# Outputs on four column tiles, values copied over the head's partitions by DMA

## The reference

```python
def step(state, inp):
    r_t, d_t, k_t, v_t, a_t, b_t = inp
    sa = jnp.einsum('bhij,bhj->bhi', state, a_t)
    state = state * d_t[:, :, None, :] + sa[..., None] * b_t[:, :, None, :] + v_t[..., None] * k_t[:, :, None, :]
    return (state, jnp.einsum('bhij,bhj->bhi', state, r_t))
```

## Time and profile before

| | |
|---|---|
| median of 3 runs | 1345.38 us (1345.16 to 1351.12) |
| profiled execution, span | 1345.0 us |
| instructions | 18208 |
| PE, PEld busy | 1145.7 us (85%), 648.0 us (48%) |
| DVE busy | 978.8 us (73%) |
| ACT busy | 708.3 us (53%) |
| POOL busy | 615.8 us (46%) |
| DMA | 12 GB/s over the span |
| mean granted TensorE clock | 0.962 |
| first `s_a` (L884), last `state` | 67.22 us, 1251.8 us |
| a chunk in the loop, from its first `s_a` to the next chunk's | 76.8 to 78.3 us |

### The profile page before, as it was taken

One profiled execution on the slowest core, in us unless ns is written; L12 is line 12 of the kernel. 1 busy time (PEld: TensorE's weight loads), 2 busy tenths in 40 slices (PEclk: granted clock), 3 DMA queues, 4 the chain that ended last, 5 costly groups with the idle time before them and its releaser, 6 DMA issues.

```text
span 1345.0 us, 18208 instructions
## 1 busy us (share of the span) xinstructions
PE 1145.7 (85%) x4848; PEld 648.0 (48%) x4848; DVE 978.8 (73%) x2366; ACT 708.3 (53%) x1087; POOL 615.8 (46%) x869
## 2 busy tenths in 40 slices
PE   3576778999898989989799979999898998989896
PEld 1244545555545545555455545455454555555432
DVE  2477888879696968879497877969587887958311
ACT  1544446466564636466464545656355655634454
POOL 0145555555455545555355544545455554545100
PEclk9888879999999989999899999999899999989998
DMA  2000000000000000000000000000000000000000
GB/s 112 0 9 17 1 16 1 4 14 8 16 1 25 1 25 0 8 16 8 16 0 24 0 24 0 8 16 0 24 0 24 0 16 0 17 1 17 0 9 16
DMA packets 7442, 16.61 MB, mean 12 GB/s; under 512 B 956, under 2 KB 956, under 8 KB 7240
## 3 DMA queue, kind: packets, MB, share of 16 engines
q1 hardware_dynamic: 7368, 15.84, 3.4%
HBM read 11.65 MB, written 4.19 MB: 12 GB/s over the span
## 4 chain that ended last, share of the span: by engine, by line
PE 40%; DVE 36%; issue 18%; ACT 4%; DMA 1%; DVEq 1%; SPq 0%; POOL 0%; ACTq 0%; POOLq 0%
DVE state L898 7%; DVE upd L894 6%; PE sa_ps L360 6%; PE o_ps L353 5%; PE fin_a L541 5%; PE pre_a L311 3%; PE pre_b L311 3%; DVE s_a L884 3%; PE fin_b L541 3%; PE vb_ps L311 3%; PE mid_ps L311 3%; PE mid_ps L495 2%; DVE kv L872 2%; DVE y L1046 2%; PE fin_a L311 1%
## 5 line engine op out<-in xcount | busy, mean ns | idle before, releaser
L1094 POOL TENSOR_TENSOR plus_kv<-state,kv 128x128 f32<-128x128 f32 x512 | 285.4, 557 | 578.5 <-DVE state L898 542.2
L360 PEld LDWEIGHTS sa_ps<-s_a,con 128*128 128x128 f32 x1024 | 174.6, 196 | 387.6 <-DVE s_a L884 332.8
L360 PE MATMUL sa_ps<-s_a,con 128*128 128x128 f32 x1024 | 233.0, 311 | 122.1 <-DVE s_a L884 114.9
L894 DVE TENSOR_TENSOR upd<-sa_ps,b_t 128x128 f32<-128x128 f32 x512 | 144.8, 283 | 179.9 <-PE sa_ps L360 179.2
L1087 POOL TENSOR_TENSOR s_r<-state,r_t 128x256 f32<-128x256 f32 x256 | 218.6, 854 | 1.0 <-DVE state L898 1.0
L898 DVE TENSOR_TENSOR state<-upd,plus_kv 128x128 f32<-128x128 f32 x512 | 153.7, 300 | 17.6
L884 DVE TENSOR_TENSOR s_a<-state,a_t 128x128 f32<-128x128 f32 x512 | 149.3, 292 | 17.7
L353 PE MATMUL o_ps<-s_r,con 128*128 128x128 f32 x1024 | 142.4, 285 | 1.5 <-POOL s_r L1087 1.5
L541 PE MATMUL fin_b<-h_e,mat 128*128 128x512 f32 x256 | 129.6, 604 | 7.6 <-ACT pick L776 6.8
L353 PEld LDWEIGHTS o_ps<-s_r,con 128*128 128x128 f32 x1024 | 131.7, 201 | 1.7 <-POOL s_r L1087 1.7
L541 PE MATMUL fin_a<-h_e,mat 128*128 128x512 f32 x256 | 122.1, 593 | 0.0
(11 more groups left out here) (185 smaller groups left out, 2021.0 us busy)
## 6 DMA issues: line engine op xcount, KB each, us to landing
x_in<-xT SPq DMA_DIRECT2D x16, 256.0 KB, 2.7
x_res<-xT SPq DMA_DIRECT2D x16, 256.0 KB, 2.8
outT<-res SPq DMA_DIRECT2D x16, 256.0 KB, 2.0
mat<-mats SPq DMA_DIRECT2D x1, 2306.0 KB
con<-consts SPq DMA_DIRECT2D x1, 840.0 KB, 4.3
hid<-b SPq DMA_DIRECT2D x3, 8.0 KB
vec<-vecs SPq DMA_DIRECT2D x1, 11.5 KB, 4.5
```

The costliest lines, as they stand in the source:

```text
L360: mm(sa_ps[:, 0:STATE], k("sum8"), s_a[:], start=True, stop=True).then_inc(s["sa"], 1)
L894: tt(ib(upd[:]), ib(sa_ps[:, 0:STATE]), over_i(b_t[c.slot][:, t * B:(t + 1) * B]), ALU.mult).then_inc(s["upd"], 1)
L1094: tt(plus_kv[:, (t % 2) * STATE:(t % 2 + 1) * STATE], st(t), kv[:, at:at + STATE], ALU.add).then_inc(s["plus_kv"], 1)
```

## The change

The partitions of everything behind the scan are ordered by value, then head (i times 16 plus h), by permuting columns and rows of the weights on the host, and the head's mean is taken off in the weights of a second form of v and no longer in `gather`.

- Outputs: `gather` becomes 32 columns wide; the matmuls of the values 2p and 2p+1 write the 32 partitions of column tile p of `o_ps`, the even value with `start`, the odd one with `stop`. All eight matmuls are in step 3 of the next quarter.
- Values: `pre` makes a centered v with channels on the partitions by one 512-column matmul (`val_scan`, made in the fill), and ACT copies it to `val_c`. SP issues, for each quarter, eight SBUF-to-SBUF DMAs, one for each value i: 16 partitions of `val_c` read eight times each, written to 128 partitions of `val_rep`, 64 KB. DVE's `kv` reads `val_rep` in SBUF. ACT's `replicate`, PE's `spread` and the waits of `vb_free` are gone. v for the bonus is made by a second 512-column matmul.

```diff
+for _name, _w in [("center", C), ("mean", C), ("mean8", C), ("center8", C), ("sum8", C), ("sum8v", C), ("ident", C),
+                  ("gather", N * 32), ("rank", 4 * E)]:
...
+        val_rep = [sb(f"val_rep{n}", N * QCOLS) for n in range(2)]
+        val_scan = sb("val_scan", C)
+        val_c = sb("val_c", COLS)
...
 # SP
+            def replicate(c, q):
+                slot, turn = q % 2, q // 2
+                free = c.count(2 * (q - 2) + 2, 2 * QUARTERS)
+                if not isinstance(free, int) or free > 0:
+                    sp.wait_ge(s["kv"], settled(sp, free))
+                if q == 0:
+                    sp.wait_ge(s["val_c"], settled(sp, c.count()))
+                for i in range(N):
+                    heads = val_c[i * H:(i + 1) * H, q * QCOLS:(q + 1) * QCOLS].unsqueeze(1).broadcast_to([H, N, QCOLS])
+                    sp.dma_start(val_rep[slot][:, i * QCOLS:(i + 1) * QCOLS], heads).then_inc(s[f"val_rep{slot}"], 16)
+
+            def pre(c):
+                yield 17
+                replicate(c, 0)
+                yield 18
+                replicate(c, 1)
+
+            def scan(c):
+                yield 1
+                replicate(c, 2)
+                yield 8
+                replicate(c, 3)
...
-            pipeline(nc.sync, fill, [(2, norm), (-1, mid), (-3, last_norm)], None, finish)
+            pipeline(nc.sync, fill, [(2, norm), (1, pre), (0, scan), (-1, mid), (-3, last_norm)], None, finish)
...
 # PE, fill
+                nc.tensor.transpose(fin_b[:, 0:C], w("W_v"), k("ident")).then_inc(s["wv_turned"], 1)
+                pe.wait_ge(s["wv_sb"], 1)
+                mm(fin_b[:, C:2 * C], val_scan[:], k("center8"), start=True, stop=True,
+                   skip_group_check=True).then_inc(s["wv_c"], 1)
+                pe.wait_ge(s["wv_sb"], 2)
...
 # PE, outputs
-                for n in range(N // 2):
-                    i = half * N // 2 + n
-                    last = mm(o_ps[:, q * QCOLS:(q + 1) * QCOLS], k("gather", i), part[:, i],
-                              start=(i == 0), stop=(i == N - 1), skip_group_check=True)
-                if half:
-                    last.then_inc(s["o"], 1)
+                for odd in range(2):
+                    for pair in range(N // 2):
+                        i = 2 * pair + odd
+                        last = mm(o_ps[32 * pair:32 * pair + 32, q * QCOLS:(q + 1) * QCOLS], k("gather", i, 32),
+                                  part[:, i], start=(odd == 0), stop=(odd == 1), skip_group_check=True)
+                last.then_inc(s["o"], 1)
...
 # PE, scan step
-                if at in (1, 2) and nxt[0].has():
...
-                    spread(*nxt, at - 1)
-                if at in (3, 4) and done[0].has():
-                    outputs(*done, at - 3)
+                if at == 3 and done[0].has():
+                    outputs(*done)
...
 # PE, pre
-                for n in range(QUARTERS):
-                    last = mm(pre_a[:, n * C:(n + 1) * C], mix["v"][:, n * QCOLS:(n + 1) * QCOLS], w("W_v"),
-                              start=(n == 0), stop=True, skip_group_check=True)
-                last.then_inc(s["v"], 1)
+                one(pre_a[:], val_scan[:], mix["v"][:], "v")
...
-                pe.wait_ge(s["val_tm"], c.count())
-                for n in range(QUARTERS):
-                    last = nc.tensor.transpose(pre_a[:, n * QCOLS:(n + 1) * QCOLS],
-                                               val_tm[c.slot][:, n * C:(n + 1) * C], k("ident"))
-                last.then_inc(s["vt"], 1)
+                pe.wait_ge(s["val_c"], c.count())
+                one(pre_a[:], w("W_v"), mix["v"][:], "val_mm")
...
 # ACT
-                if at in (0, 1) and nxt[0].has():
-                    replicate(*nxt, at)
...
-                f(val_tm[c.slot][:], pre_a[:], ACT.Identity).then_inc(s["val_tm"], 1)
+                if c.has(1):
+                    act.wait_ge(s["val_rep0"], (c + -1).count(32 * N, 32 * N))
+                    act.wait_ge(s["val_rep1"], (c + -1).count(32 * N, 32 * N))
+                f(val_c[:], pre_a[:], ACT.Identity).then_inc(s["val_c"], 1)
...
 # DVE, spread_kv
-                dve.wait_ge(s["vb"], c.count(2 * q + half + 1, 2 * QUARTERS))
+                dve.wait_ge(s[f"val_rep{q % 2}"], c.count(16 * N * (q // 2 + 1), 32 * N))
...
+                values = val_rep[q % 2][:, half * N // 2 * QCOLS:(half + 1) * N // 2 * QCOLS]
+                values = values.rearrange("p (i t b) -> p i t b", i=N // 2, t=QUARTER)
...
-                tt(part, vb_ps[:].rearrange("p (i t b) -> p i t b", i=N // 2, t=QUARTER),
+                tt(part, values,
                    keys.unsqueeze(1).broadcast_to([128, N // 2, QUARTER, B]), ALU.mult).then_inc(s["kv"], 1)
```

More of the change, by code:

```diff
@@ L194, in build @@
         res = single("res", COLS)
-        sa_ps, o_ps, vb_ps = bank("sa_ps"), bank("o_ps"), bank("vb_ps")
+        sa_ps, o_ps, var_ps = bank("sa_ps"), bank("o_ps"), bank("var_ps")
         pre_a, pre_b, mid_ps, fin_a, fin_b = (bank(n) for n in ("pre_a", "pre_b", "mid_ps", "fin_a", "fin_b"))
@@ L201, in build @@
         names = """x_in x_res stored consts_in w_in consts_ready
-            wo_turned wo_sb wo_c bo_c c0 sq0 j0 ln0 rs0 xh0 x1 x1_keep c1 sq1 j1 ln1 rs1 xh1 xn carry dx mix_w mix_a mix_k mix_v mix_r mix_g
-            w1 th_w a1 low_a k key v val_tm val_rep vt val r rec g1 th_g w2 th_d a2 th_a dec cum p inv_p
+            wo_turned wo_sb wo_c wv_turned wv_sb wv_c bo_c c0 sq0 j0 ln0 rs0 xh0 x1 x1_keep c1 sq1 j1 ln1 rs1 xh1 xn carry dx mix_w mix_a mix_k mix_v mix_r mix_g
+            w1 th_w a1 low_a k key v val_c val_rep0 val_rep1 val_mm val r rec g1 th_g w2 th_d a2 th_a dec cum p inv_p
             sqk kks nrm lnk rk kk kki b_t a_t ka_f k2 k_t r_t rkb rkb_ps bonus bonus_b g2 gate
-            state s_a sa plus_kv upd vb kv s_r o
+            state s_a sa plus_kv upd kv s_r o
             o_sb gsq gj gln grs gxh gaff gg wo x2 x2x fc fsq fj fln frs fxh xf fcarry fdx kf
@@ L329, in fill, with outputs @@
                 pe.wait_ge(s["wo_sb"], 4)
[L331 to L337, removed]
-                for n in range(N // 2):
[L339 to L348, removed]
+                nc.tensor.transpose(fin_b[:, 0:C], w("W_v"), k("ident")).then_inc(s["wv_turned"], 1)
[3 more added lines that the diff above has]
+                pe.wait_ge(s["wv_sb"], 2)
+            def outputs(c, q):
+                pe.wait_ge(s["s_r"], c.count(4 * q + 4, 4 * QUARTERS))
+                if q == 0 and c.has(1):
+                    pe.wait_ge(s["o_sb"], (c + -1).count())
                 part = s_r[:, (q % 2) * QUARTER * STATE:(q % 2 + 1) * QUARTER * STATE]
                 part = part.rearrange("p (t i b) -> p i t b", t=QUARTER, i=N)
-                for n in range(N // 2):
-                    i = half * N // 2 + n
-                    last = mm(o_ps[:, q * QCOLS:(q + 1) * QCOLS], k("gather", i), part[:, i],
-                              start=(i == 0), stop=(i == N - 1), skip_group_check=True)
-                if half:
-                    last.then_inc(s["o"], 1)
+                for odd in range(2):
[4 more added lines that the diff above has]
+                last.then_inc(s["o"], 1)
             def scan_step(c, t, stages):
@@ L471, in mid @@
                 pe.wait_ge(s["gln"], c.count())
-                pe.wait_ge(s["kv"], vb_free(c + 1, 3))
                 if c.has(2):
                     pe.wait_ge(s["lvar"], (c + -2).count())
-                one(vb_ps[:], k("mean"), sq_m[:], "fj")
+                one(var_ps[:], k("mean"), sq_m[:], "fj")
                 yield 22
-            def vb_free(scan, quarter):
-                n = scan.count(2 * quarter + 2, 2 * QUARTERS)
-                return min(n, CHUNKS * 2 * QUARTERS) if isinstance(n, int) else n
             def fin(c):
@@ L557, in last_norm @@
                 pe.wait_ge(s["lsq"], c.count())
-                pe.wait_ge(s["kv"], vb_free(c + 3, 2))
                 pe.wait_ge(s["gln"], newest_mid(c))
-                one(vb_ps[:], k("mean"), sq_f[:], "lj")
+                one(var_ps[:], k("mean"), sq_f[:], "lj")
                 yield 16
@@ L690, in pre @@
                 yield 17
[L691 removed]
+                act.wait_ge(s["val_mm"], c.count())
                 if c.has(1):
```

75 lines of the change are left out of this document (23 added, 52 removed).

## The result

The changed kernel takes 1402.46 us (median of 4 runs, 1398.08 to 1405.36) against 1345.27 for the kernel before (4 runs, 1343.45 to 1351.12): ratio 1.041, interval 1.0383 to 1.0438. It is slower, as forecast, but by 57 us in place of 25, and outside the range. Its profiled execution has a span of 1403.6 us against 1345.0, so the traces show 58.6 us.

A forecast was written before the change was run, and what follows sets the result against it. Neither TensorE (40% of the span) nor the vector engine (36%) was taken as the bound throughout; it varies by scan step. +1.65 us in 13 full chunks (21.5), plus early chunks and ends, net +25 on 1345.0: 1370 us, range 1344 to 1391.

The forecast's parts named there:

- what DVE pays: Eight `kv` steps a chunk get longer with both operands in SBUF, as GpSimd is disturbed too: 3.31 us a chunk.
- +0.44, +0.45, +0.26: Added us per step: +0.44 in steps 10, 18, 26; +0.45 in steps 11, 19, 27; +0.26 in step 3.
- the 0.33 of step 4: Step 4 falls from 1.86 us to the bare 1.53 once the outputs' second half leaves it: 0.33 us gained.
- operand source doesn't matter: Rival, 0.08: `kv` stays at 0.68 us and only PE's gains are left, -1.66 a chunk, 1320 us.
- only `kv` itself is longer: Rival, 0.17: POOL absorbs the rest, steps 10 to 27 cost 1.5 in place of 2.67 us; 1355 or 1348.
- what PE saves: Moving the outputs' second half gains 0.44 us in step 5, 0.89 in step 28 and 0.33 in step 4.
- Column tiles one behind the other: Rival, 0.11: a quarter's outputs take 1.91 us in one step, delaying steps 4 and 28; 1384 us.
- the copies: The 32 DMAs a chunk on SP's queue land in time and cost nothing; rival of copies too late, 0.04.
- TensorE's clock falls more often: Rival, 0.10: with less PE work, one more half-clock stretch a chunk costs +1 to +1.5 us; 1385 to 1390.
- the forecast's 1.65: Sum of DVE's costs and PE's gains per full chunk, +1.65 us, for chunks 2 to 14: 21.5 us.
- about +5 for 0 and 1: Chunks 0 and 1, where PE is seldom late, pay without the gains: about +5 us together.
- nothing and -1.5 were forecast: Chunk 15 changes nearly nothing; `kv` of chunk 0 no longer alternating with PE and smaller last outputs give about -1.5 us.

The follow-up runs named there:

- the filler in step 12: The changed kernel plus four 128-column float32 matmuls that nobody reads, at the end of step 12 of every chunk: 1375.96 us, ratio 1.0235.
- the run that was to remove it: The changed kernel plus unread matmuls in steps 12 (4) and 19 (6), and 3 a step from step 12 on in chunks 0 and 1: 1375.97 us.
- one part alone: Column tiles and the new partition order, with values copied as in the kernel before (ACT, PE's transposes, `kv` from PSUM): 1336.18 us, ratio 0.9925.

## Why the prediction was wrong

**Right: what DVE pays.** +0.44, +0.45, +0.26, and +0.39 for step 2 (0.38 forecast); alone the operand's move measures +3.1 and +2.8 us in chunks 3 and 4 against 3.31 less the 0.33 of step 4. The price was to be read from whole steps of the kernel before that already had such neighbours. `s_r` is 1.17 us in step 2 (mean 954 ns against 854), and `kv` is 940 ns from SBUF and 683 from PSUM with nothing else changed, but 680 from SBUF with GpSimd idle. The rule that a vector instruction with two SBUF inputs and a GpSimd instruction that reads SBUF exclude each other (the Trainium skill, "SBUF — State Buffer", "Who interferes with whom") is borne out by these numbers. The rivals "operand source doesn't matter" and "only `kv` itself is longer" have fallen.

**Right: what PE saves, in steps 5 and 28.** 0.44 and 0.89; with wide outputs both are gone. The quarter of outputs is 0.57 us and not 0.9, which nothing in the sum depended on: four column tiles ran at 1.71 / 0.57 = 3.0 times the rate of one behind the other. (The 2.38x for three tiles in the Trainium skill, "TensorE: Matmul & The Clock Gate", Part 3, lies below that; three were not run here.) The 0.33 of step 4 was right in the sum, but its account was incomplete: the narrow outputs alone give 0.12 of it (1.72 from 1.84 us), and either the longer step 3 or the transposes' absence beside them gives the whole. "Column tiles one behind the other" has fallen.

**Right: the copies** cost nothing, shown by leaving them out. Their issue was priced too low (0.33 us, measured 0.6), which nothing in the sum depended on.

**Wrong: the clock.** The step that failed is the price of TensorE's clock. The sum puts it at nothing, and the rival "TensorE's clock falls more often", at 0.10, prices it at +1 to +1.5 us a chunk, "with 1.7 us of stage matmuls doubled in each of two or three steps that have 0.5 us to spare". The mechanism was the rival's and the size was not. The stretch came about every second chunk in the middle, not in each; but it fell on steps 13 to 17, where PE is busy for 12.12 of 12.38 us. Steps 14 to 17 of chunk 9 take 3.75, 3.84, 3.04 and 3.68 us for 2.33, 2.17, 2.31 and 3.20: +4.3 at once. I had called these steps DVE-bound, since `upd` starts when DVE is free; they were bound by both engines, and one window over them would have said so. The stretches at steps 19 to 21 cost nothing: what I had assumed of steps with room holds there.

Chunks 5 to 14 together are 808.2 us against 769.9, so the mean is (38.3 - 16.5) / 10 = 2.2 us a chunk above the forecast's 1.65, where the range allowed 1.5 at most. The rival had named PE's missing work as the cause, and the runs bear that out: the outputs and transposes in front of the dense steps had kept the clock, and putting back either the outputs' second half or unread matmuls in step 12 keeps it. With the unread matmuls the kernel measures 1376, 6 us above the forecast.

**Wrong: chunks 0 to 2, by the same term.** I forecast about +5 for 0 and 1 and +1.65 for 2, and they measure +22.7. The steps that I had priced give 7.4 of it, near the forecast, and 14.8 lie in steps at a lower clock than before. Only 10 of these are shown by an experiment (the filler in step 12); for the rest the clock is read from the traces, since the run that was to remove it lengthened other steps. Chunk 15 and the ends went the other way: from chunk 15's first `s_a` to the end it is 150.3 us against 156.6, -6.3 where nothing and -1.5 were forecast, partly since step 10 of chunk 15, 3.87 us at half clock before, is 1.92.

The account of the profiled 58.6 us: start of the scan +0.5; chunks 0 to 2 +22.7; chunks 3 and 4 +3.3; chunks 5 to 14 +38.3, of it 16.5 by the steps; chunk 15 and the end -6.3. That the two halves of the change are opposite in sign is now measured: the column tiles (with their own early loss of clock) are worth -8 us, and the operand's move to SBUF +50.

## What to carry to other kernels

Before work is taken off TensorE, take windows over the stretch that follows it: where PE is busy nearly all of the time at the full clock, as in 12.12 of 12.38 us here, a half-clock stretch there costs 4 us at once, and a few unread matmuls in the thinned step (26 us here) tell at once whether that is where the time went. Then look at what the unread matmuls themselves delay, as the six of step 19 did in the kernel with the column tiles alone. An operand that moves from PSUM to SBUF for the sake of saving a copy on another engine is paid for by the vector engine and by GpSimd in every step in which both work (the one `kv` beside an idle GpSimd took 680 ns, the others 941 or more); read that price from steps of the same trace that already have two SBUF operands. And a bundle of two edits should be timed in its parts: here one part alone beats both kernels.

## What the runs showed of the hardware

- The granted clock was 0.50 from 800.77 us for 10.2 us, right behind a step in which PE had 1.35 us of work where it had 1.97 before, and it stayed there through steps in which PE was busy all the time (a window over the half-clock part of the changed kernel's chunk 9, columns as above). Four unread matmuls in step 12 prevented that, the same four in step 24 did not. The 1.35 us alone do not bring it: with PE's transposes in steps 9 and 10 the same step 12 was followed by the full clock.

```profile
800.34:811.01 10.67, 10.32 (x26) 5.24 (x26) 7.75 (x22) 3.02 (x5) 3.02 (x6) 0.52 0.00 1
```

- A half-clock stretch is free or dear by where it falls: 3.4 us of it at step 20 cost nothing, 10.2 us of it from step 13 on cost 4.3.
- The same instruction on 128x512 takes 940 to 943 ns on the mean with both operands in SBUF while GpSimd works, 680 ns with both in SBUF and GpSimd idle, and 683 with one in PSUM, as a product and as a minimum.
- Sixteen passes of 128 float32 columns on four column tiles of 32 take 0.57 us.
- A broadcasting copy of 64 KB inside SBUF lands after 2.4 us; 512 of them beside the scan cost nothing measurable (1398.8 us without, 1402.5 with).
